# Rows of 132 columns for two pictures in device memory and for the strip tiles

## The chip, the cores and the metric

One core of one Trainium2 chip runs the whole program. The metric is the device time of one execution in microseconds, the median of several runs.

## The reference, cut to what matters

Two layers on four pictures of 96 channels and 128 x 128 points. The first layer is a window attention beside a depthwise 3 x 3 convolution, mixed by a gate and projected; the second is a depthwise convolution with four taps whose filter is computed from the picture's mean.

```python
x = layernorm2d(x0, ln_w, ln_b)
qk, vs = conv1x1(x, qk_w, qk_b), conv1x1(x, vs_w, vs_b)
local = depthwise3x3(vs, depth_w) + depth_b
v1, v2 = vs[:, :48], vs[:, 48:]
q, k, v1 = roll(q, -4, -4), roll(k, -4, -4), roll(v1, -4, -4)
y = roll(attention in 8 x 8 windows, 4 heads of 12 channels, +4, +4)
y = concatenate([y, v2])
s = (y + local).mean(axis=(2, 3))
ca = sigmoid(fu2(leaky_relu(fu1(s), 0.2)))
y = conv1x1(y * ca + local * (1 - ca), proj_w, proj_b) + x0
out = depthwise, 4 taps of a masked 3 x 3, filter from mean(y)
```

## The kernel before, in words

The pictures are worked through in strips of 8 rows, 16 strips to a picture and 64 in all (`NS`, `B`). A strip holds 16 windows of 8 x 8 points. The rows of the attention's strips lie 4 rows lower than those of the output's strips, because of the roll.

There are two stages, and they run interleaved. The attention stage takes strip t: it loads x, normalises it into `xn`, makes values, keys and queries, the scores, the softmax and the attention's output, and stores two pictures in device memory: `v_img` (the value picture, 96 channels, with a zero row above and below) and `y_img` (the attention's output, 48 channels). The output stage runs 17 strips later (`LAG`): it loads strip u = t - 17 of both pictures into `vin` (10 rows with a zero column at either side), `ycat` and `x0`, adds the nine taps and the projection up in PSUM, and applies the second layer to the strip `zs`. The gate and the filter of a picture need sums over the whole picture, so at the end of each picture two strips carry extra steps (the strips with `gate` and `gated`), a chain of small products and sums that goes back and forth between VectorE and TensorE.

So the program has three kinds of strips. The first 16 run the attention alone (the functions `alone`). Then 48 strips run both stages (`strip`). The last 17 strips run the output stage alone (`last` on VectorE).

There is no scheduler: on each engine the order of the work is written out by hand, as one list of calls per strip, and semaphores with counted values do the rest. The orders that matter here:

- ScalarE (ACT), `strip` at L827: the two exponentials `exps(t, 0)`, the two copies `vs_out` of the values with their bias, `y_out(t - 1)`, `exps(t, 1)`, the two `keys`, `rsqrt`, the two `queries`, then `tap0`, `sum_x`, `first`, `values`.
- TensorE (PE), `strip` at L624: `x_transposed`, `scores_transposed(k, 0)`, `vs_of`, `y_transposed(t - 1)`, `scores_transposed(k, 1)`, `keys_queries`, `values(t, k, 0)`, `rstd_rows`, then a wait for the keys and the queries (L651, L652), `scores(1 - k, 0)` (L493), `project`, `scores(1 - k, 1)`, `values(t, k, 1)`, `project`, `v_transposed`, `project_mixed`.
- VectorE (DVE), `strip` at L1175: `finish`, statistics, five tap sums `mix`, `divide`, `normalise`, `maxima`, taps of the second layer `l1`.
- GpSimd (POOL), `to_image` at L410: eight small copies that turn the values from window order into rows (`vrow`), and one for the edge columns.
- SyncE (SP) issues all the DMAs.

The names that the change touches: `load_x` (L265) loads x rolled by four columns, so that each half strip takes two DMAs, one of 124 columns and one of 4. `windows` (L463) reads windows out of `xn`. `yq` holds the attention's output in window order with 2 x 48 channels for two groups of windows; `y_transposed` (L513) transposes it to 96 partitions, group 0 on partitions 0 to 47 and group 1 on 48 to 95; `y_out` (L757) copies that to `ybuf` with two instructions, one for each `wi`, each with a sum for the picture's mean into `ystat`; `store_y` (L282) writes `ybuf` to `y_img` with four DMAs in runs of 32 columns. `load_strip` (L292) reads `y_img` back with two DMAs, rolled by four columns. `mean_y` (L1051) sums `ystat`, and the product with `fold` (L667, issued by L574) adds the two groups of partitions. Two things on PE wait for `y_out`: `values(t, k, 0)` through `y1_done` (L525), and nothing else; but `exps(t, 1)` and all that follows it on ACT stand behind `y_out` in ACT's list.

Of the kernel before, what the change touches and what calls it, by code (L numbers as in the profile page):

```python
# [31 lines left out]
SH = WS // 2  # L32
# [12 lines left out]
VW = HD + 1  # L45

# [32 lines left out]
def program(nc, x, out, w):  # L79
    ctx = ExitStack()  # L80
    with ctx:
# [40 lines left out]
        xn = sb("xn", [C, WS, W])  # L122
# [7 lines left out]
        idle = sb("idle", [C, 1])  # L130
        rec = sb("rec", [128, 2, 16])
        yq = sb("yq", [128, 4, 2, A])
        vrow = sb("vrow", [C, 2, WS, W])
        ybuf = sb("ybuf", [C, 2, WS, 2, 4 * WS])

        vstat = sb("vstat", [C, 2 * (B * NS + 2)])
        ystat = sb("ystat", [C, 2 * B * NS])
# [14 lines left out]
        vin = sb("vin", [C, 2, WS + 2, W + 2])  # L152
        ycat = sb("ycat", [C, 2, WS, W])
        x0 = sb("x0", [C, 2, WS, W])
        mb = sb("mixed", [C, 2, WS, W])
# [3 lines left out]
        v_img = nc.dram_tensor("v_img", (B + 1, C, H + 2, W), F32, kind="Internal").ap()  # L159
        y_img = nc.dram_tensor("y_img", (B, A, H, W), F32, kind="Internal").ap()  # L160
# [34 lines left out]
        xn_done = sem("xn_done")  # L195
        xsum_done = sem("xsum_done")
# [36 lines left out]
        N_MID, MID_STEPS, MID_PE = 28 + len(PE_TAPS), 6, 7  # L233
# [21 lines left out]
        def _(sp):  # L255
# [26 lines left out]
            def store_y(s, par):  # L282
                b, i = image_of(s)
                at = [held(rows_of(i, c)) for c in range(2)]
                sp.wait_ge(y1_done, 2 * (s + 1))
                for c in range(2):
                    rows = y_img[b, :, bass.ds(at[c], 4), :].rearrange("c r (w g x) -> c r w g x", w=2, g=2)
                    for g in range(2):
                        sp.dma_start(rows[:, :, :, g, :],
                                     ybuf[g * A:(g + 1) * A, par, 4 * c:4 * c + 4, :, :]).then_inc(y_stored[par], 16)  # L290

            def load_strip(u, par, prev, gate):  # L292

                b, j = image_of(u)
                before, top, below = held(u - 1), held(j * WS), held(j * WS + 1)
                if prev:
                    sp.wait_ge(z_done, before)
                sp.dma_start(vin[:, par, :, 1:1 + W], v_img[b, :, bass.ds(top, WS + 2), :]).then_inc(vin_loaded[par], 16)
                sp.dma_start(ycat[A:C, par, :, :], v_img[b, A:C, bass.ds(below, WS), :]).then_inc(ycat_loaded[par], 16)
                rows = y_img[b, :, bass.ds(top, WS), :]  # L300
                if gate is not None:
                    sp.wait_ge(y_stored[1], FREE + 64 * (NS // 2) * (gate + 1))
                sp.dma_start(ycat[0:A, par, :, SH:W], rows[:, :, 0:W - SH]).then_inc(ycat_loaded[par], 16)
                sp.dma_start(ycat[0:A, par, :, 0:SH], rows[:, :, W - SH:W]).then_inc(ycat_loaded[par], 16)
# [16 lines left out]
            for b in range(B):  # L321
                for row in (0, H + 1):
                    sp.dma_start(v_img[b, :, row, :], zs[:, 0, 0:W]).then_inc(rim_stored, 16)
# [8 lines left out]
            def strip(h, k, attend=True, y=True, ahead=False, prev=False, older=False, gate=None):  # L332
# [4 lines left out]
                if gate is not None:  # L337
                    sp.wait_ge(y_stored[0], FREE + 64 * (NS // 2) * (gate + 1))
                    sp.wait_ge(v_stored[0], 32 * ((gate + 1) * (NS // 2) + 1))
                    sp.wait_ge(v_stored[1], 32 * (gate + 1) * (NS // 2))  # L340
                    for at, row in ((0, H), (1, 1)):
                        sp.dma_start(erow[:, at, :], v_img[gate, :, row, :]).then_inc(erow_loaded, 16)
# [50 lines left out]
        def _(pool):  # L393
            for at, value in ((0, LN_EPS), (1, BN_EPS)):
                nc.gpsimd.memset(eps[:, at:at + 1], value).then_inc(eps_set, 1)
            for t in (w_qk[:], place[:], vd[:], edge[:], idle[:], zs[:], q_scale[:],
                      vin[:, 0, :, 0], vin[:, 0, :, W + 1], vin[:, 1, :, 0], vin[:, 1, :, W + 1]):
# [12 lines left out]
            def to_image(s, par, free):  # L410
# [5 lines left out]
                for c in range(2):  # L416
# [5 lines left out]
                    put(rows[:, :, SH:SH + W // 2], of[:, 0])  # L422
# [889 lines left out]
```

## Time and profile before, and how to read it

| | us |
|---|---|
| median of 3 runs | 1599.65 (1597.12 to 1601.26) |
| the profiled execution, its own time | 1606.61 |
| span of the profiled execution | 1604.8 |
| busy in it: PE, DVE, ACT, POOL | 1524.8, 1335.9, 791.9, 222.7 |
| mean granted clock of TensorE, share of the full 2.4 GHz | 0.977 |

The profile shows one execution. Busy times are sums over the span; the kernel's stages have different limits, so a share is only of use for a stage. A row of the timeline gives the start in us from the span's beginning, the time it covers, the engine, the line, the operation with its output and inputs, and how many instructions are merged (x4); in brackets stands the idle time of the engine before it and what ended that. SPq is SyncE's queue, its rows are the issues of DMAs. PEld is the load of weights into TensorE. ACTIVATION_READ_ACCUMULATOR is the second half of an ACT instruction that also sums.

### The profile page before, as it was taken

The page shows a single profiled execution, that of the slowest core. Times are in us where ns is not written, and L with a number is a line of the kernel's source. Part 1 is how long each engine was busy: PE and PEld are TensorE (multiplying, and loading weights), DVE is VectorE, ACT ScalarE, POOL GpSimd, SP SyncE. Part 2 cuts the span into 40 slices and gives each one's busy share as a digit, 9 for nine tenths or more (in the row PEclk, how much of TensorE's full clock was granted, in tenths as well). Part 3 has the DMA queues.
Part 4 walks back from the last instruction along what each step waited for, and adds up shares of the span by engine and source line. Part 5 has one row for each costly group of instructions (what it writes and reads, how often), then busy time and mean ns, then how long its engine had stood idle before and what let it go on. Part 6 is the DMA issues. An engine that isn't in the chain of part 4 may idle for free.

```text
span 1604.8 us, 34488 instructions
## 1 busy us (share of the span) xinstructions
PE 1524.8 (95%) x10619; PEld 932.8 (58%) x10619; DVE 1335.9 (83%) x2450; ACT 791.9 (49%) x1819; POOL 222.7 (14%) x675
## 2 busy tenths in 40 slices
PE   5999999899999999999999999989999999969997
PEld 3676767666656666556656665556566665523332
DVE  3565656559999999889999999889999999889998
ACT  2555555435555555536555556545555565512221
POOL 1111111101111111201111111111111111100000
PEclk9999999869999999989999999999999999989999
DMA  2232222426655665455566655664566555657874
GB/s 57 52 71 56 68 59 65 85 58 125 132 112 108 124 128 126 110 98 118 115 115 130 123 117 110 121 121 92 118 133 123 112 111 121 134 104 157 161 161 109
DMA packets 360943, 174.15 MB, mean 109 GB/s; under 512 B 267760, under 2 KB 333064, under 8 KB 360904
## 3 DMA queue, kind: packets, MB, share of 16 engines
q1 hardware_dynamic: 360904, 173.69, 52.6%
q8 instruction: 17, 0.28, 0.1%
q14 instruction: 22, 0.18, 0.0%
HBM read 108.85 MB, written 63.70 MB: 108 GB/s over the span
## 4 chain that ended last, share of the span: by engine, by line
PE 85%; DVE 8%; issue 3%; ACT 1%; DMA 1%; SPq 0%; DVEq 0%; ACTq 0%
PE banks_g L586 14%; PE banks_s L497 8%; PE banks_g L472 8%; PE banks_t L533 7%; PE banks_a L533 7%; PE banks_g L480 6%; PE banks_g L593 6%; PE banks_t L505 6%; PE banks_g L588 6%; PE banks_t L459 4%; PE banks_t L586 3%; PE banks_a L447 2%; PE banks_a L486 2%; DVE zs L1143 2%; PE banks_a L517 2%
## 5 line engine op out<-in xcount | busy, mean ns | idle before, releaser
L1120 DVE SCALAR_TENSOR_TENSOR mixed<-vin,c_pack,mixed 96x1024 f32<-96x1024 f32 x352 | 453.8, 1289 | 6.4
L586 PE MATMUL banks_g<-vin,proj_t 96*96 96x512 f32 x512 | 250.1, 616 | 3.6 <-DVE st L1094 3.6
L1131 DVE SCALAR_TENSOR_TENSOR oo<-zs,l_w,oo 96x1024 f32<-96x1024 f32 x192 | 245.5, 1279 | 8.9 <-ACT oo L805 3.3
L755 ACT ACTIVATE vd<-banks_a 64x192 f32<-64x192 f32 x260 | 86.9, 334 | 307.3 <-PE banks_a L486 302.4
L922 DVE TENSOR_REDUCE mx<-banks_s 128x8 f32<-128x512 f32 x260 | 167.1, 684 | 39.7 <-PE banks_s L497 36.3
L769 ACT ACTIVATE pt<-banks_t 128x512 f32<-128x512 f32 x256 | 138.6, 593 | 97.4 <-PE banks_t L505 97.4
L420 POOL COPY vrow<-vw 96x16 f32<-96x16 f32 (+2 forms) x520 | 177.3, 390 | 0.0
L415 POOL TENSOR_TENSOR idle<-idle 96x1 f32<-96x1 f32 x65 | 13.4, 207 | 1163.1 <-ACT vw L746 1163.1
L497 PEld LDWEIGHTS banks_s<-km,qd 64*128 64x128 f32 x2080 | 132.6, 195 | 56.1 <-DVE mx L922 38.3
L497 PE MATMUL banks_s<-km,qd 64*128 64x128 f32 x2080 | 157.8, 293 | 4.8 <-DVE mx L922 3.3
L795 ACT ACTIVATE mixed<-vin,c_pack 96x1024 f32<-96x1024 f32 x64 | 73.5, 1149 | 166.8 <-DMA vin<-v_img 166.8
L505 PE MATMUL banks_t<-qd,km 64*128 64x128 f32 x2048 | 152.2, 289 | 1.4 <-DMA qd<-nmx 1.4
L893 DVE BATCH_NORM_STATS2 bn<-banks_a 128x6 f32<-128x96 f32 x528 | 98.7, 247 | 58.0 <-PE banks_a L447 56.2
L533 PEld LDWEIGHTS banks_a<-vd,pt 128*128 128x128 f32 x1024 | 120.8, 194 | 41.1 <-issue 41.1
L472 PE MATMUL banks_g<-xn,c_pack 96*96 96x512 f32 x260 | 133.5, 638 | 9.2 <-DVE zs L1143 8.3
L505 PEld LDWEIGHTS banks_t<-qd,km 64*128 64x128 f32 x2048 | 127.4, 191 | 19.1 <-issue 8.7
L805 ACT ACTIVATE oo<-zs,c_pack,l_w 96x1024 f32<-96x1024 f32 x64 | 79.1, 1235 | 118.9 <-DVE zs L1143 118.9
L586 PEld LDWEIGHTS banks_g<-vin,proj_t 96*96 96x96 f32 x512 | 78.8, 167 | 98.3 <-issue 89.5
L533 PE MATMUL banks_t<-vd,pt 128*128 128x52 f32 x1024 | 128.9, 280 | 0.0
L480 PE MATMUL banks_g<-xn,w_qk 96*32 96x512 f32 x1040 | 128.6, 613 | 0.0
L533 PE MATMUL banks_a<-vd,pt 128*128 128x52 f32 x1024 | 127.3, 278 | 0.0
L533 PEld LDWEIGHTS banks_t<-vd,pt 128*128 128x128 f32 x1024 | 120.7, 194 | 7.9 <-issue 0.2
(134 smaller groups left out, 1909.7 us busy)
## 6 DMA issues: line engine op xcount, KB each, us to landing
vin<-v_img SPq DMA_DIRECT2D x64, 480.0 KB, 5.7
v_img<-vrow SPq DMA_DIRECT2D x130, 192.0 KB, 2.2
xc<-in_x SPq DMA_DIRECT2D x134, 186.0 KB, 5.6
x<-in_x SPq DMA_DIRECT2D x64, 384.0 KB, 7.0
out<-oo SPq DMA_DIRECT2D x64, 384.0 KB, 3.0
y_img<-ybuf SPq DMA_DIRECT2D x256, 48.0 KB, 1.7
ycat<-v_img SPq DMA_DIRECT2D x64, 192.0 KB, 5.4
ycat<-y_img SPq DMA_DIRECT2D x64, 186.0 KB, 5.5
```

The lines of the kernel that those rows point to most:

```text
L420: nc.gpsimd.tensor_copy(dst.rearrange("c r (p x) -> c p r x", x=min(WS, src.shape[-1])), src).then_inc(vrow_done, 1)
L472: mm(banks_g[:C, w, :], wvs[:], windows(w), start=True, stop=True).then_inc(vs_done, 1)
L480: last = mm(banks_g[q0:q0 + 32, at, :], w_qk[:, kind, t, :], windows(w), start=True, stop=True, tile_position=(0, q0))
L497: last = mm(banks_s[:, t, e * 128:(e + 1) * 128], operand(qd, t, k, p), operand(km, t, k, p), start=True, stop=True, tile_position=(64 * t ...
L505: last = mm(banks_t[:, n, e * 128:(e + 1) * 128], operand(km, n, k, p), operand(qd, n, k, p), start=True, stop=True, tile_position=(64 * n ...
L533: last = mm(bank[:, at:at + 52], pt[:, 2 * half + n, e * 128:(e + 1) * 128], vd[:, k, 4 * half + e, n, :, :, :].rearrange("k w h d -> k (w ...
L586: mm(z, proj_t[:, n, :], vin[:, par, at:at + 4, 1 + dw:1 + dw + W], start=n == 0, stop=False)
L769: fn(pt[:, 2 * r + n, :], banks_t[:, n, :], ACT.Exp).then_inc(pt_done, 1)
L893: last = v.bn_stats(bn6[:, c, j, :], ps_ln[:, j * C:(j + 1) * C])
L922: v.tensor_reduce(mx[:, n, :, 4 * r:4 * r + 4].rearrange("q h e -> q e h"), banks_s[:, n, :].rearrange("q (e h k) -> q e h k", h=2, k=K), ...
L1120: v.scalar_tensor_tensor(out=mb[:, par, :, :], in0=vin[:, par, 1 + dh:1 + dh + WS, 1 + dw:1 + dw + W], scalar=depth_w[:, DVE_TAPS[m]:DVE_T ...
L1131: v.scalar_tensor_tensor(out=oo[:, par, :, :], in0=zs[:, at:at + WS, 1 + dw:1 + dw + W], scalar=l1_w[:, n:n + 1], in1=oo[:, par, :, :], op ...
```

## The change

Rows get a pitch of 132 columns (`PITCH = W + SH`) in `xn`, `vrow`, `ybuf`, `vin`, `ycat`, `mixed` and in the two pictures in device memory, so that a strip tile and the rows that are stored and loaded have the same layout, and one channel of a DMA is one contiguous run.

- x is loaded as it lies, with one DMA for each half strip. GpSimd copies the first four columns of `xn` behind the last (`wrap`, new), and `windows` reads from column 4 on. `vs_of` waits for that copy.
- The value picture's row has a zero column ahead and three behind; `vin` is loaded with one DMA of whole rows, and its columns are no longer set to zero by themselves. `vrow`, `yq`, `ystat` and a new tile `nil` are set to zero at the start.
- `yq` gets 64 columns for each group, so that the transposed output has group 0 on partitions 0 to 47 and group 1 on 64 to 111. `y_out` copies it with four instructions, two for each group, all to partitions 0 to 47 of `ybuf`, in turned columns, and a fifth for four columns that wrap round.
- `store_y` takes two DMAs in place of four, the load of `y_img` one in place of two.
- `ystat` has four sums for each strip on 48 partitions, and the product with `fold` goes; `mean_y`, `squeeze_in` and `leaky` count one step less to PE.

The core of the diff:

```diff
+PITCH = W + SH
+YO = 5
             def load_x(b, i, c):
-                rows, strip = x[b, :, bass.ds(rows_of(i, c), 4), :], chunk(xc[:, c, :])
-                sp.dma_start(strip[:, :, 0:W - SH], rows[:, :, SH:W]).then_inc(x_loaded[c], 16)
-                sp.dma_start(strip[:, :, W - SH:W], rows[:, :, 0:SH]).then_inc(x_loaded[c], 16)
+                sp.dma_start(chunk(xc[:, c, :]), x[b, :, bass.ds(rows_of(i, c), 4), :]).then_inc(x_loaded[c], 16)
...
                 for c in range(2):
-                    rows = y_img[b, :, bass.ds(at[c], 4), :].rearrange("c r (w g x) -> c r w g x", w=2, g=2)
-                    for g in range(2):
-                        sp.dma_start(rows[:, :, :, g, :],
-                                     ybuf[g * A:(g + 1) * A, par, 4 * c:4 * c + 4, :, :]).then_inc(y_stored[par], 16)
+                    sp.dma_start(y_img[b, :, bass.ds(at[c], 4), :],
+                                 ybuf[:, par, 4 * c:4 * c + 4, :]).then_inc(y_stored[par], 16)
...
-                sp.dma_start(ycat[0:A, par, :, SH:W], rows[:, :, 0:W - SH]).then_inc(ycat_loaded[par], 16)
-                sp.dma_start(ycat[0:A, par, :, 0:SH], rows[:, :, W - SH:W]).then_inc(ycat_loaded[par], 16)
+                sp.dma_start(ycat[0:A, par, :, :], y_img[b, :, bass.ds(top, WS), :]).then_inc(ycat_loaded[par], 16)
...
-                      vin[:, 0, :, 0], vin[:, 0, :, W + 1], vin[:, 1, :, 0], vin[:, 1, :, W + 1]):
+                      vrow[:], yq[:], ystat[:], nil[:]):
...
+            def wrap(s):
+                pool.wait_ge(xn_done, 2 * (s + 1))
+                nc.gpsimd.tensor_tensor(xn[:, :, W:PITCH], xn[:, :, 0:SH], nil[:], ALU.add).then_inc(xw_done, 1)
...
             def vs_of(s):
-                pe.wait_ge(xn_done, 2 * (s + 1))
+                pe.wait_ge(xw_done, s + 1)
...
-                    last = nc.tensor.transpose(ps_o[:C, e * 128:(e + 1) * 128],
+                    last = nc.tensor.transpose(ps_o[:, e * 128:(e + 1) * 128],
...
             def y_out(t, par, before):
                 act.wait_ge(yt_done, t + 1)
-                src = ps_o[:C, :].rearrange("c (e w r x) -> c e w r x", e=4, w=2, x=WS)
-                for wi in range(2):
-                    dst = ybuf[:, par, :, wi, :].rearrange("c r (e x) -> c e r x", x=WS)
-                    fn(dst, src[:, :, wi, :, :], ACT.Copy,
-                       accum_out=ystat[:, bass.ds(2 * t + wi, 1)]).then_inc(y1_done, 1)
+                for g in range(2):
+                    src = ps_o[64 * g:64 * g + A, :].rearrange("c (e w r x) -> c e w r x", e=4, w=2, x=WS)
+                    for wi in range(2):
+                        at = SH + wi * W // 2 + g * W // 4
+                        dst = ybuf[:, par, :, at:at + W // 4].rearrange("c r (e x) -> c e r x", x=WS)
+                        fn(dst, src[:, :, wi, :, :], ACT.Copy,
+                           accum_out=ystat[0:A, bass.ds(4 * t + 2 * g + wi, 1)]).then_inc(y1_done, 1)
+                fn(ybuf[:, par, :, 0:SH], src[:, 3, 1, :, SH:WS], ACT.Copy).then_inc(y1_done, 1)
...
-                if gate is not None:
-                    one_column(gate, fold[:], st[:, 0:1], 0, C, 1)
```

## Rows read from the trace of the kernel before

**Rows 1.** The page, part 4: the chain that ended last, by engine

```profile
PE 85%; DVE 8%; issue 3%; ACT 1%; DMA 1%; SPq 0%; DVEq 0%; ACTq 0%
```

**Rows 2.** Busy time by stage: stretch, length, each engine, PE's clock, DMA share, GB/s

```profile
40.00:296.00 256.00, 238.31 (x2308) 180.13 (x2306) 151.24 (x428) 137.59 (x376) 35.30 (x160) 1.00 0.27 62
296.00:350.00 54.00, 49.98 (x307) 34.86 (x306) 28.27 (x90) 22.91 (x55) 5.43 (x20) 0.65 0.43 87
350.00:660.00 310.00, 307.87 (x2249) 188.86 (x2250) 284.08 (x491) 174.51 (x399) 52.97 (x140) 1.00 0.57 117
...
1435.00:1605.00 170.00, 159.80 (x379) 60.68 (x377) 156.74 (x128) 37.37 (x37) 0.00 (x0) 0.98 0.70 145
```

**Rows 3.** Timeline of ACT in one strip with both stages

```profile
883.40 0.37 ACT L763 ACTIVATE ybuf<-banks_a 96x256 f32<-96x256 f32 x1
883.66 0.19 ACT L763 ACTIVATION_READ_ACCUMULATOR ybuf<-banks_a  x1
883.75 0.37 ACT L763 ACTIVATE ybuf<-banks_a 96x256 f32<-96x256 f32 x1
...
884.18 1.08 ACT L769 ACTIVATE pt<-banks_t 128x512 f32<-128x512 f32 x2
885.68 1.45 ACT L733 ACTIVATE km<-banks_g,k_bias,k_scale 128x512 f32<-128x512 f32 x2 [0.41 <-PE banks_g L480]
...
887.54 1.43 ACT L739 ACTIVATE qd<-banks_g,q_bias,q_scale 128x512 f32<-128x512 f32 x2
```

**Rows 4.** Timeline of PE in the same strip, before and after ACT's queries

```profile
886.40 1.99 PE L533 MATMUL banks_a<-vd,pt 128*128 128x52 f32 x16
...
889.19 1.16 PE L497 MATMUL banks_s<-km,qd 64*128 64x128 f32 x16
```

**Rows 5.** The page, part 2: DMA packets of the whole span

```profile
DMA packets 360943, 174.15 MB, mean 109 GB/s; under 512 B 267760, under 2 KB 333064, under 8 KB 360904
```

**Rows 6.** Timeline of SP's queue at the start

```profile
1.48 0.42 SPq L267 DMA_DIRECT2D xc<-in_x  x1
...
2.98 0.48 SPq L268 DMA_DIRECT2D xc<-in_x  x1
```

**Rows 7.** The chain of waits at the start: start, length, what

```profile
3.50 2.52 DMA ln_pack<-in_ln_pack
...
10.26 0.15 DVE place L963
```

**Rows 8.** Timeline of POOL at the start

```profile
2.73 1.94 POOL L398 MEMSET zs<- 96x2210 f32 x1
...
5.46 0.53 POOL L407 MEMSET q_scale<- 32x1 f32 x4
```

**Rows 9.** Timeline of all engines: from the normalised strip to its first reader

```profile
864.64 1.26 POOL L426 COPY ecol<-vw 96x16 f32 x1
...
868.12 1.28 DVE L914 TENSOR_TENSOR xn<-banks_t,xc 96x512 f32<-96x512 f32 x2
...
880.65 1.96 PE L472 MATMUL banks_g<-xn,c_pack 96*96 96x512 f32 x4
```

**Rows 10.** Groups of instructions by line and shape: count, busy us, mean ns

```profile
L769 ACT ACTIVATE pt<-banks_t 128x512 f32<-128x512 f32 x256 | 138.6, 593 | 97.4 <-PE banks_t L505 97.4
...
L755 ACT ACTIVATE vd<-banks_a 64x192 f32<-64x192 f32 x260 | 86.9, 334 | 307.3 <-PE banks_a L486 302.4
```

**Rows 11.** Timeline of ACT in a strip of the attention alone, and four copies merged

```profile
201.21 1.41 ACT L755 ACTIVATE vd<-banks_a 64x192 f32<-64x192 f32 x4 [5.48 <-PE banks_a L486]
...
204.97 1.08 ACT L769 ACTIVATE pt<-banks_t 128x512 f32<-128x512 f32 x2 [0.16 <-PE banks_t L505]
206.85 1.45 ACT L739 ACTIVATE qd<-banks_g,q_bias,q_scale 128x512 f32<-128x512 f32 x2 [0.79 <-PE banks_g L480]
...
209.36 1.06 ACT L769 ACTIVATE pt<-banks_t 128x512 f32<-128x512 f32 x2
```

**Rows 12.** Timeline of PE: the end of an attention strip, and the last picture's gate

```profile
210.57 1.04 PE L459 MATMUL banks_t<-ident,rstd 128*96 128x128 f32 x8 [1.01 <-ACT pt L769]
...
1412.62 0.48 PE L574 MATMUL banks_s<-st,c_pack 96*96 96x1 f32 x2 [6.83 <-DVE st L1053]
```

More of the change, by code:

```diff
@@ L284, in store_y, with strip_of @@
                 at = [held(rows_of(i, c)) for c in range(2)]
[L285 removed]
+                sp.wait_ge(y1_done, YO * (s + 1))
                 for c in range(2):
[L287 to L290 removed]
+                    sp.dma_start(y_img[b, :, bass.ds(at[c], 4), :],
+                                 ybuf[:, par, 4 * c:4 * c + 4, :]).then_inc(y_stored[par], 16)
             def load_strip(u, par, prev, gate):
                 b, j = image_of(u)
[L295 removed]
+                before, top = held(u - 1), held(j * WS)
+                first, below = held(j * WS * PITCH + 1), held(j * WS * PITCH + PITCH + 1)
+                def strip_of(c0, c1, at):
+                    flat = v_img[b, c0:c1, :, :].rearrange("c r x -> c (r x)")
+                    return flat[:, bass.ds(at, WS * PITCH)].rearrange("c (r x) -> c r x", x=PITCH)
                 if prev:
                     sp.wait_ge(z_done, before)
[L298 to L300 removed]
+                sp.dma_start(vin[:C, par, :, :], v_img[b, :, bass.ds(top, WS + 2), :]).then_inc(vin_loaded[par], 16)
+                sp.dma_start(ycat[A:C, par, :, :], strip_of(A, C, below)).then_inc(ycat_loaded[par], 16)
                 if gate is not None:
[L302 to L304 removed]
+                    sp.wait_ge(y_stored[1], FREE + 32 * (NS // 2) * (gate + 1))
+                sp.dma_start(ycat[0:A, par, :, :], y_img[b, :, bass.ds(top, WS), :]).then_inc(ycat_loaded[par], 16)
                 if prev:
@@ L337, in strip @@
                 if gate is not None:
-                    sp.wait_ge(y_stored[0], FREE + 64 * (NS // 2) * (gate + 1))
+                    sp.wait_ge(y_stored[0], FREE + 32 * (NS // 2) * (gate + 1))
                     sp.wait_ge(v_stored[0], 32 * ((gate + 1) * (NS // 2) + 1))
@@ L341, in strip @@
                     for at, row in ((0, H), (1, 1)):
-                        sp.dma_start(erow[:, at, :], v_img[gate, :, row, :]).then_inc(erow_loaded, 16)
+                        sp.dma_start(erow[:, at, :], v_img[gate, :, row, 1:1 + W]).then_inc(erow_loaded, 16)
                 if y:
@@ L524, in values @@
                     if not first:
-                        pe.wait_ge(y1_done, 2 * t)
+                        pe.wait_ge(y1_done, YO * t)
                 else:
@@ L587, in project @@
                        start=n == 0, stop=False)
-                mm(z, proj_c[:], ycat[:, par, 4 * c:4 * c + 4, :], start=False, stop=False)
+                mm(z, proj_c[:], ycat[:, par, 4 * c:4 * c + 4, 0:W], start=False, stop=False)
             def project_mixed(u, par, last):
@@ L592, in project_mixed @@
                 for c in range(2):
-                    done = mm(z_bank(par, last)[:C, c, :], proj_m[:], mb[:, par, 4 * c:4 * c + 4, :], start=False, stop=True)
+                    done = mm(z_bank(par, last)[:C, c, :], proj_m[:], mb[:, par, 4 * c:4 * c + 4, 0:W], start=False, stop=True)
                 done.then_inc(z_done, 1)
@@ L672, in strip @@
                 if gate is not None:
-                    one_column(gate, fu1T[:], st[:, 5:6], 1, R, 2)
+                    one_column(gate, fu1T[:], st[:, 5:6], 1, R, 1)
                 if gated is not None:
@@ L683, in strip @@
                 if gate is not None:
-                    one_column(gate, fu2T[:], tr[:, 1:2], 2, C, 3)
+                    one_column(gate, fu2T[:], tr[:, 1:2], 2, C, 2)
             alone(0, 0, y=False)
@@ L1051, in mean_y @@
             def mean_y(b):
-                dve.wait_ge(y1_done, 2 * NS * (b + 1))
-                to_pe(b, v.tensor_reduce(s(0), ystat[:, bass.ds(2 * NS * b, 2 * NS)], AX.X, ALU.add))
+                dve.wait_ge(y1_done, YO * NS * (b + 1))
+                step(v.tensor_reduce(s(0), ystat[:, bass.ds(4 * NS * b, 4 * NS)], AX.X, ALU.add))
             def squeeze_in(b):
                 settle(b)
-                dve.wait_ge(mid_pe, MID_PE * b + 1)
-                step(v.tensor_scalar(s(4), one[:C, 0:1], s(8), 1.0 / PX, ALU.add, ALU.mult))
+                step(v.tensor_scalar(s(4), s(0), s(8), 1.0 / PX, ALU.add, ALU.mult))
                 settle(b)
```

76 lines of the change are left out of this document (42 added, 34 removed).

## The prediction

> **What bounds the kernel now.** I read the chain of waits first, summed by engine: TensorE (PE) carries 85% of it, DMA 1%, ScalarE (ACT) 1% [rows 1]. Then busy time by stage [rows 2], because a share of the span mixes stages. From 40 to 296 us attention runs alone, PE is busy for 238 of 256 us, and the chain leaves it in each strip for a detour over VectorE (DVE) and ACT. From 350 to 660 us both stages run: PE is busy for 307.87 of 310 us, DVE for 284. Fourteen strips fit there, and two more stretches of fourteen look the same, so 42 strips have PE full. In the tail from 1435 us DVE is busy for 157 of 170 us: its eight passes over a strip set the pace. DMA engines are busy for a quarter to 0.7 of each stage, and nowhere the limit.
>
> Third, the timeline of one of those 42 strips, to see what PE barely gets in time. ACT has a share of only 56% there, yet works in a fixed order. In it `y_out` ends, `exps(t, 1)` follows at once, then the keys start after 0.41 us of idle time, then the queries end at 887.54 + 1.43 = 888.97 [rows 3]. PE's scores, which read them, start at 889.19 [rows 4], 0.22 us later, with PE's preceding work just done. So ACT's list has some slack ahead of the keys and next to none behind them.
>
> **The change part by part.**
>
> *DMA.* 267,760 of 360,943 packets are under 512 bytes [rows 5]; x's pieces, `ybuf`'s runs of 128 bytes and the rolled load of `y_img` make up most of these, and they become runs of about 2 to 5 KB. DMA time will fall a good deal. Worth: 0 in the steady stages, because no strip waits there for a landing on its chain (DMA 1%, [rows 1]); the cover is PE's and DVE's own work. SP issues five DMAs fewer in a strip; nothing that SP issues is late.
>
> *The start.* SP issues four loads of x, then the pack on which the chain stands at 3.50 us [rows 6, 7]. Two loads fewer at (2.98 - 1.48) / 3 = 0.50 us each: -1.0 us. POOL's new zeros are 2112 + 512 + 256 + 32 elements a partition; by the 2210 elements in 1.94 us that is some 2.5 us, so POOL's set-up ends at 5.99 + 2.5 = 8.5 us [rows 8]. DVE first asks for it at 10.26 - 1.0 = 9.3 us [rows 7]: covered by 0.8 us. In the first strip `wrap` stands openly between normalise and `vs_of`: 0.2 us for a small POOL instruction and one more semaphore, estimate +0.3. Sum: -0.7 us.
>
> *`wrap` in the other strips.* `xn` is ready at 868.12 + 1.28 = 869.40 and read at 880.65 [rows 9]: 11.2 us for one small copy behind `to_image`. Even the slowest small POOL copy, 1.26 us beside DVE's passes [rows 9], fits nine times. Cost 0.
>
> *PE.* Four transposes load 128 columns where they loaded 96. Bounds: nothing, because each streams 128 columns as before and the load runs beside it, up to a few hundredths each. I take 0. Reading windows from column 4 of a 132 pitch: the taps already read shifted rows of 130 at the normal pace; 0.
>
> *`y_out` on ACT.* Here the cost lies. Today two copies, each with a read of its sum, take 883.75 - 883.40 = 0.35 us a pair [rows 3], although the two parts last 0.37 and 0.19: each instruction starts about 0.1 us before the one ahead has ended. After: four pairs and a copy of 32 elements. I take a pair on 48 partitions to cost what one on 96 does, since a copy of 64 x 192 lasts 0.334 [rows 10], near the 0.37 less 64 elements: 2 x 0.355 = 0.71 more. The small copy: two exponentials of 512 elements last 1.08 together [rows 3] and one 0.593 [rows 10], so a step of 0.49; the 256 of `ybuf` step 0.26; that is 0.9 ns an element, and 0.07 for 32 elements. Sum with full overlap 0.78 us.
>
> Does the overlap hold? The only ACT instructions here that change their partitions from one to the next are the four of L755, from and to halves of 64: each lasts 0.334, four take 1.41 [rows 10, 11], so a step of 0.36. The overlap of 0.1 is gone and 0.025 of gap is added: 0.12 each. In the new `y_out` the source moves from partition 0 to 64 between the groups and back before `exps`; the target stays. L755 changes its target each time, so it doesn't say which of the two counts. Ends: 0.78 us (only targets count), and, with no overlap anywhere, 4 x (0.37 + 0.20 + 0.05) + 0.2 - 0.71 = 1.98. I take two drains, 0.78 + 0.24 = 1.02, as L755 is the nearest row.
>
> Slack ahead of the keys: 0.41 idle, 0.1 for the overlap that a chained instruction has, and 0.07 that `exps` waits today: 0.58. So keys and queries come 1.02 - 0.58 = 0.44 us later. Of the 0.22 us between the queries' end and PE's start, 0.15 is the step from ACT's end to PE in the nearest row (209.36 + 1.06 to 210.57, [rows 11, 12]); slack 0.07 to 0.22, I take 0.12. PE is late by 0.44 - 0.12 = 0.32 us in each strip. Nothing gives it back: DVE's `finish`, and with it the next strip, starts from PE's last product. 42 x 0.32 = +13.4 us. `y1_done` costs nothing: y ends at about 884.1 + 1.0, its reader starts at 886.40 [rows 4].
>
> *The same in attention alone.* There `exps(t, 0)` waits 0.16 and the queries 0.79 us [rows 11], with 0.1 of overlap about the 1.02; PE idles 1.01 later in the strip anyway [rows 12]. Cost 0.
>
> *`fold`.* At the last gate PE waits 6.83 us for `mean_y` before `fold` [rows 12], and `project` stands behind it. Afterwards `project` runs in that gap, but DVE still carries the chain, and PE idles longer ahead of its next product. Between -2 and +2; I take 0.
>
> Sum: -0.7 + 13.4 = +12.7 us, on the profiled execution 1606.61 + 12.7 = 1619.3. That execution is 7.0 us above the median of the runs, 1599.65; the forecast for the median is **1612 us**.
>
> **The rivals.**
>
> *Full overlap, no difference.* Only targets count, ACT's block grows by 0.78, the queries come 0.20 later, PE 0.08: 42 x 0.08 - 0.7 = +2.7, **1602 us**. For it: target and source both move in L755's middle step, and its step is no longer than the other two. Against it: both move in none of the rows without the target. The Trainium skill, "ScalarE: Activation LUTs", section "What ACT_TABLE_LOAD costs", states that back-to-back ACTIVATEs overlap by about 93 ns, with no exception for partitions; by that rule this rival holds. The pair in rows 3 agrees with it, the four copies in rows 11 don't.
>
> *More drains.* The read of a sum may have partitions of its own, so that each step from group 1's source to its sum drains. Six drains: 0.78 + 0.72 - 0.58 - 0.12 = 0.80 a strip, +33 us, **1632**; no overlap at all: 1.98 - 0.70 = 1.28, +53, **1653**. Against the latter: 96 and 128 partitions alternate now without a drain.
>
> *Faster, through the clock.* Around the first gate, 296 to 350 us, PE's granted clock averages 0.65 [rows 2], so part of that stretch runs at 1.2 GHz, after waits of PE in the gate's chain. At the full clock it would take up to 0.35 x 54 = 19 us less. One step less in the chain could keep the clock up; it decides if the granted clock there rises above 0.9. With the full-overlap cost: 1602 - 19 = **1583**. Against it: `fold` isn't what PE waits for there, and the wait ahead of the drop is DVE's maxima. In the attention stage an idle 1 us in each strip leaves the clock at 1.00.
>
> *It doesn't do what it says*: if the packets stayed small, time would be as forecast, as DMA isn't in the sum.
>
> **How the numbers follow.** A measurement of this kernel can tell 0.3%, 4.8 us, from no change. Two drains (about +12.7) 0.44; full overlap 0.34, nearly all within 0.3%; more drains 0.14; faster through clock or gates 0.07, the small rest spread. So faster 0.08, same 0.34, slower 0.58. The range reaches from the full-overlap case with all its slack, 1599 - 1 = 1598, to six drains, 1633; left out are the clock case and no overlap at all. The forecast's own range, by the slack's ends (0.07 to 0.22), is 1608 to 1615.
>
> **What would show it.** In a steady strip: five y copies in about 1.7 us; no idle time ahead of the keys (0.41 before); scores starting 0.15 to 0.2 after the queries' end with an idle PE ahead of them; the strip longer by 0.3 us; PE's share from 350 to 660 us below 99%. Packets under 512 bytes fall to under a tenth. `wrap` done ten us ahead of its reader. Wrong I am if the keys still wait for PE, if steady strips keep their length, or if the difference lies at the gates.

## The result, and the profile after

The kernel after takes 1612.76 us (median of 7 runs, 1608.79 to 1620.32), the kernel before beside it 1603.62 us: ratio 1.0063, 95% interval 1.0035 to 1.0091. A second comparison, told below, gave 1615.26 against 1599.90 us: 1.0091, interval 1.0066 to 1.0116. So the change costs 9 to 15 us, more than the 0.3% that can be told from no change.

The page of the kernel after: the DMA packets and the chain that ended last.

```profile
DMA packets 72143, 177.10 MB, mean 109 GB/s; under 512 B 12176, under 2 KB 16040, under 8 KB 72104
...
PE 85%; DVE 9%; issue 4%; ACT 1%; DMA 1%; SPq 0%; DVEq 0%; ACTq 0%; POOL 0%; POOLq 0%
```

The change does what it says: four fifths fewer packets, and those under 512 bytes fall from 267,760 to 12,176 [rows 5]. DMA's share of the chain stayed at 1% [rows 1].

Busy time by stage of the kernel after (columns as in rows 2):

```profile
40.00:296.00 256.00, 238.11 (x2319) 180.10 (x2317) 152.32 (x432) 151.84 (x453) 40.19 (x176) 1.00 0.22 63
...
350.00:660.00 310.00, 303.73 (x2222) 187.28 (x2221) 278.57 (x481) 185.82 (x467) 64.74 (x154) 1.00 0.46 117
```

In the attention alone ACT has 14 us more work and PE's figure is as in [rows 2]. In the stretch with both stages ACT has 11 us more, the DMA share fell from 0.57 to 0.46, and PE lost 4 of its 308 busy us. What PE waits for there is one view further, the sum of its waits by what ended them (total us, times, longest). First the kernel before, then the kernel after, 350 to 660 us:

```profile
PE banks_g L472 <- DVE zs L1143: 2.1, 7, 0.3
```

```profile
PE banks_s L511 <- issue: 4.1, 14, 0.3
PE banks_g L486 <- DVE zs L1157: 2.1, 7, 0.3
```

Fourteen new waits of 0.29 us, one in each strip, ahead of the scores; the old one, for `zs` in every second strip, is unchanged. "Issue" names no releaser; the timeline does. It shows ACT of the kernel after in one such strip, with the lines of PE and POOL that are used here and below:

```profile
887.85 0.36 ACT L777 ACTIVATE ybuf<-banks_a 48x256 f32<-48x256 f32 x1
...
888.21 0.37 ACT L777 ACTIVATE ybuf<-banks_a 48x256 f32<-48x256 f32 x1
888.47 0.20 ACT L777 ACTIVATION_READ_ACCUMULATOR ybuf<-banks_a  x1
888.69 0.38 ACT L777 ACTIVATE ybuf<-banks_a 48x256 f32<-48x256 f32 x1
...
889.07 0.37 ACT L777 ACTIVATE ybuf<-banks_a 48x256 f32<-48x256 f32 x1
...
889.43 0.18 ACT L779 ACTIVATE ybuf<-banks_a 48x32 f32<-48x32 f32 x1
889.64 1.08 ACT L784 ACTIVATE pt<-banks_t 128x512 f32<-128x512 f32 x2
890.61 1.45 ACT L745 ACTIVATE km<-banks_g,k_bias,k_scale 128x512 f32<-128x512 f32 x2
...
892.47 1.43 ACT L751 ACTIVATE qd<-banks_g,q_bias,q_scale 128x512 f32<-128x512 f32 x2
...
894.00 1.16 PE L511 MATMUL banks_s<-km,qd 64*128 64x128 f32 x16 [0.29 <-issue]
...
896.04 0.25 POOL L436 TENSOR_TENSOR xn<-xn,nil 96x32 f32<-96x32 f32 x1 [3.58 <-DVE xn L929]
...
907.86 1.93 PE L486 MATMUL banks_g<-xn,c_pack 96*96 96x512 f32 x4 [0.31 <-DVE zs L1157]
```

Read it beside [rows 3, 4]. The copies follow each other by 0.36 us while they read the same group of partitions; from the second to the third, where the source moves from partition 0 to 64, the step is 0.48, and the third begins after the read ahead of it has ended (888.47 + 0.20 = 888.67). The same between the small copy (889.43 + 0.18 = 889.61) and the exponentials at 889.64. The keys no longer wait for PE: the 0.41 us ahead of them are gone. The queries end at 893.90, and PE's scores start 0.10 us later after an idle 0.29. (The last line is a product that waits for `zs` by 0.31, the old wait.)

### The profile page after: what moved, and what is told of

Read it like the earlier page. It is cut to its first block, busy times and chain, and to the rows that moved or that the text cites. A ratio compares the mean times of both kernels' runs of the same rounds, so it can differ in the third digit from the quotient of the medians.

```text
span 1618.5 us, 34138 instructions
## 1 busy us (share of the span) xinstructions
PE 1526.5 (94%) x10611; PEld 933.6 (58%) x10611; DVE 1332.2 (82%) x2450; ACT 847.7 (52%) x2139; POOL 269.4 (17%) x741
## 2 busy tenths in 40 slices
DMA packets 72143, 177.10 MB, mean 109 GB/s; under 512 B 12176, under 2 KB 16040, under 8 KB 72104
## 4 chain that ended last, share of the span: by engine, by line
PE 85%; DVE 9%; issue 4%; ACT 1%; DMA 1%; SPq 0%; DVEq 0%; ACTq 0%; POOL 0%; POOLq 0%
PE banks_g L600 14%; PE banks_s L511 8%; PE banks_g L486 8%; PE banks_t L547 7%; PE banks_a L547 7%; PE banks_g L494 6%; PE banks_g L607 6%; PE banks_t L519 6%; PE banks_g L602 6%; PE banks_t L473 4%; PE banks_t L600 3%; PE banks_a L461 2%; PE banks_a L500 2%; DVE zs L1157 2%; PE banks_a L531 2%
## 5 line engine op out<-in xcount | busy, mean ns | idle before, releaser
L424 POOL COPY vrow<-vw 96x16 f32<-96x16 f32 (+2 forms) x520 | 182.5, 405 | 0.0
```

Of the source, the lines that this page charges most:

```text
L424: nc.gpsimd.tensor_copy(dst.rearrange("c r (p x) -> c p r x", x=min(WS, src.shape[-1])), src).then_inc(vrow_done, 1)
```

## Where the time came from

A strip is measured here from the start of its first scores to the same two strips on, since strips alternate. Kernel before: 889.19 [rows 4] and, two strips on, 933.60; kernel after: 894.00 and 939.15.

```profile
933.60 1.16 PE L497 MATMUL banks_s<-km,qd 64*128 64x128 f32 x16
```

```profile
939.15 1.16 PE L511 MATMUL banks_s<-km,qd 64*128 64x128 f32 x16 [0.29 <-issue]
```

So 44.41 us for a pair before and 45.15 after: +0.37 a strip (22.04 and 22.37 became 22.40 and 22.74). The same starts, taken over the whole span, split the difference. Two pairs of profiled executions are shown, the first from the comparison above, the second from both kernels profiled again (runs `e8_before_again` and `e9_after_again` below):

| stretch | before | after | diff. | before again | after again | diff. |
|---|---|---|---|---|---|---|
| start to first strip's scores | 32.06 | 31.67 | -0.39 | 31.87 | 31.54 | -0.33 |
| from there to second strip's scores | 16.69 | 15.53 | -1.16 | 15.59 | 16.83 | +1.24 |
| attention alone, 15 strips | 239.35 | 239.34 | 0.0 | 239.45 | 239.37 | -0.1 |
| first gate, 3 strips | 78.74 | 77.90 | -0.8 | 68.47 | 68.30 | -0.2 |
| steady, 39 strips | 865.37 | 879.96 | **+14.6** | 865.46 | 880.00 | **+14.5** |
| other gates, 6 strips | 156.86 | 158.08 | +1.2 | 156.78 | 157.78 | +1.0 |
| rest | 215.72 | 216.02 | +0.3 | 215.68 | 216.57 | +0.9 |
| span | 1604.8 | 1618.5 | +13.7 | 1593.3 | 1610.4 | +17.1 |

What stands out in both pairs is the steady strips: 39 by 0.374 us. The second row differs by 1.1 to 1.3 us between two executions of the same kernel, so it says nothing of the change; in that strip PE's products still come down to the shorter time of later strips (16 of L497 take 2.08 us in the first strip's scores, 1.16 in the second's).

## The experiments

The theory (A): `y_out` on ACT is the whole cost; its steps lose their overlap where the source's partitions change (a drain, as the prediction calls it), and what of the longer block doesn't fit into ACT's slack of 0.7 us is paid in each strip. Rivals: rows, loads and packets matter; any longer block is paid in full; the wait lies elsewhere.

**One part alone.** `e1_y_only`: of the change, the attention's output alone (y's tiles and picture, `y_out`, `fold` no longer applied).

```diff
-                src = ps_o[:C, :].rearrange("c (e w r x) -> c e w r x", e=4, w=2, x=WS)
-                for wi in range(2):
...
+                for g in range(2):
+                    src = ps_o[64 * g:64 * g + A, :].rearrange("c (e w r x) -> c e w r x", e=4, w=2, x=WS)
+                    for wi in range(2):
...
+                fn(ybuf[:, par, :, 0:SH], src[:, 3, 1, :, SH:WS], ACT.Copy).then_inc(y1_done, 1)
```

> The kernel before with the change's part for y alone (y_out, yq, ybuf, y_img, ycat, no fold); x is loaded rolled and v_img and vin keep their old rows. Theory A (ACT's longer y block, two drains in it, makes keys and queries late, and PE waits for the queries): a pair of strips with both stages takes 45.1 us as after the change, not 44.4; keys start without idle time ahead of them; 13 to 16 us above before (ratio about 1.009). Theory B (the cost comes from GpSimd's new copy ahead of vs_of, or from reading and writing rows of 132): 44.4 us for a pair, ratio 1.000.

Measured: 1610.93 against 1601.09 us, ratio 1.0073 (1.0045 to 1.0101). Scores two strips apart in it:

```profile
884.90 1.16 PE L499 MATMUL banks_s<-km,qd 64*128 64x128 f32 x16 [0.29 <-issue]
...
930.05 1.16 PE L499 MATMUL banks_s<-km,qd 64*128 64x128 f32 x16 [0.29 <-issue]
```

45.15 us, the pace of the whole change. `e2_x_and_v`: the rest of the change without y.

```diff
-YO = 5
+YO = 2
...
-                                 ybuf[:, par, 4 * c:4 * c + 4, :]).then_inc(y_stored[par], 16)
+                                     ybuf[g * A:(g + 1) * A, par, 4 * c:4 * c + 4, :, :]).then_inc(y_stored[par], 16)
```

> The change without its part for y: x loaded as it lies with GpSimd's copy, v_img, vin, vrow and mixed with rows of 132, y as before. Theory A: 44.4 us for a pair of strips with both stages, as before; 1 to 3 us below before from the start (two loads of x fewer ahead of the first product), ratio 0.998 to 1.000. Theory B: 45.1 us for a pair, ratio about 1.008.

Measured: 1604.66 us, ratio 1.0025 (0.9997 to 1.0053).

```profile
876.32 1.16 PE L515 MATMUL banks_s<-km,qd 64*128 64x128 f32 x16
...
920.74 1.16 PE L515 MATMUL banks_s<-km,qd 64*128 64x128 f32 x16
```

44.42 us, the pace of before. The y part is the whole loss. The gain of 1 to 3 us that A expected of the rest isn't seen in the median; its execution ended 3.75 us later than the one before (219.47 us after the last strip's scores). That was asked of x alone, below.

**The drains alone.** `e3_same_half` is the kernel after with both groups read from partitions 0 to 47; it leaves out half of the attention's output. All counts, sizes and targets stay.

```diff
-                    src = ps_o[64 * g:64 * g + A, :].rearrange("c (e w r x) -> c e w r x", e=4, w=2, x=WS)
+                    src = ps_o[0:A, :].rearrange("c (e w r x) -> c e w r x", e=4, w=2, x=WS)
```

> The changed kernel, but y_out reads both groups from partitions 0 to 47 (the second group's columns are then a copy of the first's, so that half of the attention's output is left out). The same five instructions, no change of partitions between them. Theory A: the two gaps of 24 ns and the lost overlap go, the y block takes 0.24 us less, PE waits 0.24 us less in a strip: a pair takes 44.7 us, the time lies 9 to 10 us below the changed kernel (ratio to before 1.000 to 1.003). If only the number of instructions counts: 45.1 us for a pair, ratio to before 1.006.

Measured: 1597.79 us, ratio 0.9985 (0.9958 to 1.0013). ACT's timeline and PE's scores in it:

```profile
895.00 0.37 ACT L777 ACTIVATE ybuf<-banks_a 48x256 f32<-48x256 f32 x1
...
895.36 0.37 ACT L777 ACTIVATE ybuf<-banks_a 48x256 f32<-48x256 f32 x1
...
896.07 0.19 ACT L779 ACTIVATE ybuf<-banks_a 48x32 f32<-48x32 f32 x1
896.14 1.07 ACT L784 ACTIVATE pt<-banks_t 128x512 f32<-128x512 f32 x2
```

```profile
878.06 1.16 PE L511 MATMUL banks_s<-km,qd 64*128 64x128 f32 x16
...
922.61 1.16 PE L511 MATMUL banks_s<-km,qd 64*128 64x128 f32 x16
```

The second group now follows the first by 0.36, the exponentials follow the small copy by 0.07, and the pair of strips takes 44.55 us: 0.07 a strip over before, where the full-overlap rival had 0.08. So five narrow copies cost nearly nothing in the strip; the other 0.30 is the two changes of partition. The 3 us that 0.07 makes over the 39 strips don't show in the median, which lies 3 us below that of the kernel before (the interval ends at 1.0013, where 1.0019 was due).

`e4_turns` takes the groups in turn, so that the source moves four times instead of twice.

```diff
-                for g in range(2):
-                    src = ps_o[64 * g:64 * g + A, :].rearrange("c (e w r x) -> c e w r x", e=4, w=2, x=WS)
-                    for wi in range(2):
+                for wi in range(2):
+                    for g in range(2):
+                        src = ps_o[64 * g:64 * g + A, :].rearrange("c (e w r x) -> c e w r x", e=4, w=2, x=WS)
```

> The changed kernel with the four copies of y_out in another order: group 0, group 1, group 0, group 1. The same instructions and the same result, but the source changes its partitions four times in place of two. Theory A: 0.24 us more in the y block, a pair of strips takes 45.6 us, 10 us above the changed kernel (ratio to before about 1.012). If only the number of instructions counts: 45.1 us for a pair and 1.006.

Measured: 1627.97 us, ratio 1.0156 (1.0100 to 1.0212). ACT's timeline and PE's scores:

```profile
886.20 0.36 ACT L777 ACTIVATE ybuf<-banks_a 48x256 f32<-48x256 f32 x1
...
886.68 0.38 ACT L777 ACTIVATE ybuf<-banks_a 48x256 f32<-48x256 f32 x1
...
887.18 0.38 ACT L777 ACTIVATE ybuf<-banks_a 48x256 f32<-48x256 f32 x1
...
887.68 0.38 ACT L777 ACTIVATE ybuf<-banks_a 48x256 f32<-48x256 f32 x1
```

```profile
892.63 1.16 PE L511 MATMUL banks_s<-km,qd 64*128 64x128 f32 x16 [0.31 <-issue]
...
938.34 1.16 PE L511 MATMUL banks_s<-km,qd 64*128 64x128 f32 x16 [0.31 <-issue]
```

Steps of 0.48 to 0.50 at each move, and 45.71 us for the pair: two more drains cost 0.28 a strip over the kernel after, 0.14 each.

**The slack.** `e5_twice` is the kernel before with its two copies done twice, the second time into a spare tile: a longer block without a change of partitions.

```diff
+                for wi in range(2):
+                    fn(again[:, wi, :].rearrange("c (e r x) -> c e r x", e=4, x=WS), src[:, :, wi, :, :], ACT.Copy,
+                       accum_out=spare[:, bass.ds(2 * t + wi, 1)]).then_inc(y1_done, 1)
```

> The kernel before, with the two copies of y_out done a second time into a spare tile: four pairs on 96 partitions and no change of the source's partitions. It leaves nothing of the computation out. Theory A (only the lost overlap at a change of the source's partitions makes the strip longer; four pairs alone fit into ACT's slack): the block grows by 2 x 0.355 = 0.71 us, 0.58 + 0.12 of it lie in the slack, so a strip grows by 0.01 us, 22.05 and 22.38 us, the idle time ahead of the keys is 0, and the whole gains or loses under 1 us. Theory B (any longer block of ACT is paid in full): +0.71 x 42 = +30 us. Theory C (the slack ahead of the keys is the 0.41 us alone that the trace shows, and the 0.12 behind them): 0.71 - 0.53 = 0.18 in a strip, +7.6 us.

Measured: 1601.22 against 1604.75 us, ratio 0.9985 (0.9954 to 1.0015).

```profile
899.08 0.37 ACT L765 ACTIVATE ybuf<-banks_a 96x256 f32<-96x256 f32 x1
...
900.51 1.09 ACT L774 ACTIVATE pt<-banks_t 128x512 f32<-128x512 f32 x2
```

```profile
882.50 1.16 PE L499 MATMUL banks_s<-km,qd 64*128 64x128 f32 x16
...
926.91 1.16 PE L499 MATMUL banks_s<-km,qd 64*128 64x128 f32 x16
```

44.41 us, as before, though `y_out` lasts 0.72 us more (899.08 to 900.51, 1.43, against the 0.71 of two pairs) and no idle time is left ahead of the keys. Theory B's +30 us and C's +7.6 are out. The slack is about 0.71 us.

**The rest.** `e6_x_only`: the kernel before with x loaded in whole rows and turned by GpSimd.

```diff
-                sp.dma_start(strip[:, :, 0:W - SH], rows[:, :, SH:W]).then_inc(x_loaded[c], 16)
-                sp.dma_start(strip[:, :, W - SH:W], rows[:, :, 0:SH]).then_inc(x_loaded[c], 16)
+                sp.dma_start(chunk(xc[:, c, :]), x[b, :, bass.ds(rows_of(i, c), 4), :]).then_inc(x_loaded[c], 16)
```

> The kernel before with x's part of the change alone (x loaded in whole rows, turned by GpSimd in its normalised tile). Theory A: steady strips as before, 22.04 and 22.37 us, three stretches of 13 strips at 288.4 to 288.6 us; the first strip's scores earlier by 1.5 to 1.9 us as in the change and in the run without y's part; the end 215.7 and gates 78.2 to 78.7 as before. Sum -1 to -2 us. Rival: x's whole rows load the tail, and the end is 219 us as in the run without y's part (219.47): then the sum is +2 us.

Measured: 1600.29 us, ratio 0.9976 (0.9952 to 1.0000), strips of 22.04 and 22.37, end 218.1 us. The 46.84, 48.75 and 47.46 us that the next expectation calls the first strip's scores are the second strip's; the first strip's start at 31.28 us here. It was timed again:

> The kernel before with x's part of the change alone, timed in more rounds, to see whether it beats both kernels. By the traces its steady strips are those of before and its first strip's scores come 0.6 to 1.9 us earlier (46.84 us against 48.75 and 47.46 in two looks at before): a ratio of 0.9988 to 0.9996, which is within 0.3% and not told from no change. A ratio whose interval lies wholly below 0.998 would say that something else is gained.

Measured: 1599.81 us, ratio 1.0000 (0.9983 to 1.0017), first strip's scores at 31.31, second strip's at 48.03, end 215.67. So the same kernel's first scores come at the same time to 0.03 us, while the second strip's move by 1.2 us and its end by 2.4 from one execution to another. The late end of `e2_x_and_v` needs no effect of the edit (`e5_twice`, with x loaded as before, ended 219.36 us after the last scores), and the 0.24% of `e6_x_only` didn't come again. What x's part does give is 0.6 to 0.8 us at the first scores (31.28 and 31.31 against 32.06 and 31.87), too little for a median to show; of that the whole change has 0.33 to 0.39 (table above), and what takes the rest isn't located.

`e7_wrap_by_pool`: the kernel after with the small fifth copy done by GpSimd.

```diff
-                fn(ybuf[:, par, :, 0:SH], src[:, 3, 1, :, SH:WS], ACT.Copy).then_inc(y1_done, 1)
...
+                nc.gpsimd.tensor_tensor(ybuf[:, par, :, 0:SH], ybuf[:, par, :, W:PITCH], nil[:A], ALU.add).then_inc(yw_done, 1)
```

> The kernel after, with the fifth copy of y_out (the wrap columns) taken from ACT and done by GpSimd in ybuf; the two changes of the source's partitions stay. Theory A (the small copy costs its step under overlap, 0.07 us, and the two drains stay): strips of 22.33 and 22.67 us, against 22.40 and 22.74; 42 x 0.07 = 3 us less than the kernel after. Rival (the second drain belongs to the small copy, whose step to the exponentials is 0.21 us in the trace): strips of 22.20 and 22.54, 8 us less. GpSimd's later end of y (some 2.5 us) is waited for by nobody in a steady strip.

Measured: 1611.45 us, ratio 1.0058 (1.0027 to 1.0089).

```profile
885.07 1.16 PE L520 MATMUL banks_s<-km,qd 64*128 64x128 f32 x16 [0.21 <-issue]
...
930.07 1.16 PE L520 MATMUL banks_s<-km,qd 64*128 64x128 f32 x16 [0.21 <-issue]
```

45.00 us a pair, 0.08 a strip less than the kernel after, as A had it: the small copy is worth its step of 0.07, and the drain behind it stays, whichever copy stands there.

**The kernels once more.** Both unchanged, to see what belongs to the execution.

> The kernel before, profiled once more. Open is whether the time around the first gate belongs to the kernel or to the execution: the strip there took 30.63 us with a granted clock of 0.50 from 320 to 340 us in the profile before, 20.5 to 21.4 us with a clock of 0.73 to 1.00 in the four experiments so far. If to the execution, this look may show either, and a look at 21 us settles it; the steady strips are 22.04 and 22.37 us in any case. If to the kernel, it is 30 to 31 us again.

Measured: 1595.11 us in one run.

> The kernel after, profiled and timed once more. The three stretches of 13 steady strips grow by 4.8 to 5.0 us each in the profile (14.6 in all) and the start gives 1.6 back: a ratio of about 1 + 13 / 1602 = 1.008; the medians so far say 1.0063 with an interval from 1.0035 to 1.0091. The strip at the first gate took 29.04 us in the profile after; if its clock belongs to the execution, this look may show 20 to 26, as the kernel before did when it was profiled again (30.63, then 20.55). Steady strips of 22.40 and 22.74 us in any case.

Measured: 1615.26 against 1599.90 us, ratio 1.0091 (1.0066 to 1.0116). The 1.6 us at the start didn't come again: the first strip's scores were 0.33 us earlier, the second strip's 0.91 later. The clock at the first gate, 330 to 340 us, from busy time by stage: before, before again, after, after again.

```profile
330.00:340.00 10.00, 10.00 (x54) 6.57 (x54) 5.54 (x14) 5.94 (x16) 2.91 (x9) 0.50 0.77 162
```

```profile
330.00:340.00 10.00, 10.00 (x78) 7.03 (x78) 8.50 (x16) 3.95 (x9) 0.00 (x0) 1.00 0.99 203
```

```profile
330.00:340.00 10.00, 10.00 (x50) 6.40 (x50) 6.11 (x15) 6.12 (x13) 0.38 (x4) 0.50 0.72 184
```

```profile
330.00:340.00 10.00, 10.00 (x80) 7.29 (x80) 7.97 (x14) 4.41 (x10) 0.92 (x2) 1.00 0.83 208
```

Both kernels show both levels there, 1.2 and 2.4 GHz, and the strip at the gate goes with it: 30.63 and 20.55 us before, 29.04 and 21.36 after. So up to 10 us there belong to the execution. Spans of two single executions can't be compared to better than that. The attention alone and the 39 steady strips can: they repeated to 0.1 us in both kernels (in `e7_wrap_by_pool` one of the three steady stretches ran 1.2 us longer than the other two).

**A repair.** If only the place of the block costs time, it should be free where ACT stands idle. `e11_y_first` is the kernel after with the last strip's y moved ahead, on PE and on ACT.

```diff
                 if attend:
+                    if y:
+                        y_transposed(t - 1)
                     x_transposed(t + 2, 0)
...
+                if y:
+                    y_out(t - 1, 1 - k, h - 1 + k)
                 if attend:
                     exps(t, 0)
                     vs_out(t + 1, 0)
                     vs_out(t + 1, 1)
-                if y:
-                    y_out(t - 1, 1 - k, h - 1 + k)
-                if attend:
                     exps(t, 1)
```

> The kernel after with the last strip's y moved forward in the strips that run both stages: on PE its four transposes stand ahead of the first x_transposed, on ACT y_out stands ahead of exps(t, 0), where ACT sat idle for 1.91 us. All five copies and both changes of the source's partitions stay. Theory A (the drains cost time only because the block stood between the values and the exponentials, with 0.71 us of slack): the block still lasts 1.7 to 1.8 us, but it fills ACT's idle time; keys wait for PE again by about 0.4 us, strips are 22.04 to 22.15 and 22.37 to 22.5, the three stretches of 13 take 288.4 to 290 us each, and the ratio is 0.998 to 1.002. Rival (the exponentials that follow y_out come later by more than PE's slack behind them, 0.4 us, or PE's shifted transposes wait for the values' copies): strips keep 22.4 and 22.74 or more, and the ratio stays at 1.006 to 1.009.

Measured: 1591.75 against 1604.88 us, ratio 0.9919 (0.9892 to 0.9945): faster than both kernels. ACT's timeline, PE's scores and busy time by stage:

```profile
896.41 0.38 ACT L779 ACTIVATE ybuf<-banks_a 48x256 f32<-48x256 f32 x1 [1.10 <-PE banks_a L531]
...
898.22 1.08 ACT L786 ACTIVATE pt<-banks_t 128x512 f32<-128x512 f32 x2
...
902.13 1.45 ACT L747 ACTIVATE km<-banks_g,k_bias,k_scale 128x512 f32<-128x512 f32 x2 [0.41 <-PE banks_g L494]
```

```profile
883.62 1.16 PE L511 MATMUL banks_s<-km,qd 64*128 64x128 f32 x16
...
927.67 1.16 PE L511 MATMUL banks_s<-km,qd 64*128 64x128 f32 x16
```

```profile
350.00:660.00 310.00, 310.00 (x2271) 190.62 (x2271) 285.27 (x494) 187.31 (x469) 59.89 (x154) 1.00 0.47 120
```

The block is as long as in the kernel after, 1.81 us (896.41 to 898.22), the keys wait for PE by 0.41 again, and the drains cost nothing. The pair takes 44.05 us, 0.36 less than before: A had expected no more than before's pace, and 0.998 for the ratio at best. The list of PE's waits is empty in this stretch. The 0.3 us for `zs` in every second strip is gone too, since the y transposes (0.6 us, which don't need `zs`) now stand ahead of the product that does. Of the 13 us between the medians 6.5 lie in the 39 steady strips (858.9 against 865.4 us) and 2.5 in the six strips of the later gates (154.3 against 156.9); the rest isn't located, and the kernel before's own median went from 1599.90 to 1604.88 us between the comparisons here. The gain isn't the change's doing as far as this goes, so the same move was put into the kernel before.

> The kernel before with the same move of the last strip's y (transposes first on PE, y_out first on ACT), none of the change. In the run before this one the move took away two waits of PE: the 0.29 us in every strip that the change had added, and the 0.3 us for zs in every second strip, which the kernel before has too. Theory A (the two waits are independent; with both gone PE is the bound and the change itself is worth only its start): strips of 22.02 us throughout, stretches of 13 strips at 286.3 us, 39 x (22.205 - 22.02) = 7 us less than before, a ratio of 0.992 to 0.996, not more than 2 us above the run before this one. Rival (the larger gain, a ratio of 0.992 where 7 us of steady strips give 0.9955, belongs to the change's wider rows once ACT is out of the way): the ratio here is 0.995 to 0.998 and its interval lies above 0.992.

Measured: 1595.18 against 1600.61 us, ratio 0.9958 (0.9939 to 0.9977).

```profile
881.69 1.16 PE L497 MATMUL banks_s<-km,qd 64*128 64x128 f32 x16
...
925.76 1.16 PE L497 MATMUL banks_s<-km,qd 64*128 64x128 f32 x16
```

44.07 us a pair: the faster pace is the move's. Over 39 strips the two moved kernels differ by 0.6 us (859.5 against 858.9). The medians differ by 3.4 us, more than A's 2, and the ratio lies in the ranges of both theories, so whether the wider rows are worth something once ACT is out of the way stays open.

## Why the prediction was right

*What bounds the kernel*: right for the steady strips, and with one omission. PE's 307.87 of 310 us [rows 2] were read as full. The missing 2.13 us are the seven waits for `zs`, and they could be had: 6 us over the 39 steady strips, as the last two runs show.

*`y_out` on ACT*: the mechanism as forecast, two drains. Five copies with full overlap were put at +0.78 us and measured 0.79 (894.64 to 896.14 in `e3_same_half`, 1.50, against the 0.71 of two pairs). A drain was put at 0.12, from L755's steps; here it is 0.14 to 0.15. So the block grew by 1.08 instead of 1.02 (887.85 to 889.64, 1.79).

*The slack* was put at 0.58 + 0.12 = 0.70 and is 0.71: `e5_twice` adds 0.72 and loses under 0.01 a strip, `e3_same_half` adds 0.79 and loses 0.07, the kernel after adds 1.08 and loses 0.37. `e7_wrap_by_pool` adds 1.00 and loses 0.30, `e4_turns` adds 1.35 and loses 0.65. Five kernels, one number, 0.70 to 0.72. The 0.12 between the queries and PE is the 0.22 before less the 0.10 after; the prediction chose it between 0.07 and 0.22 with no row for it, so that it fits to 0.01 is partly luck, and its sign of 0.15 to 0.2 us at that place came out as 0.10.

*The strip*: +0.32 forecast, +0.37 measured; the 0.05 are the two drains' price, the term that was too small. It made 39 x 0.374 = 14.6 us, the forecast's 42 x 0.32 = 13.4. The six strips at the later gates gave 1.0 to 1.2.

*The start* was put at -0.7 and measured -0.39 and -0.33, by the first strip's scores in the two pairs of executions. Two loads fewer bring VectorE's first step on the pack 0.80 us earlier, where 1.0 was forecast (10.26 in [rows 7], 9.46 after); `wrap` takes 0.40 back, where 0.3 was forecast: PE waits 1.27 us for it, against 0.87 for the normalised strip before. First the kernel before, then the kernel after, its chain and its timeline:

```profile
18.16 3.70 PE L472 MATMUL banks_g<-xn,c_pack 96*96 96x512 f32 x4 [0.87 <-DVE xn L914]
...
32.06 2.08 PE L497 MATMUL banks_s<-km,qd 64*128 64x128 f32 x16
```

```profile
9.46 0.15 DVE place L978
```

```profile
17.76 3.70 PE L486 MATMUL banks_g<-xn,c_pack 96*96 96x512 f32 x4 [1.27 <-POOL xn L436]
...
31.67 2.08 PE L511 MATMUL banks_s<-km,qd 64*128 64x128 f32 x16
```

So the sign was right and the size half; it is 0.3 us of 1600.

*What was put at 0.* The attention alone: 239.34 against 239.35 us, although ACT does 14 us more. `wrap`: POOL ends one at 896.04 + 0.25 = 896.29 and PE reads it at 907.86, 11.6 us later. DMA: its share of the steady stretch fell by a fifth, from 0.57 to 0.46, and with x and v alone changed the pace stayed at 44.42 us a pair. PE's four transposes of the output take 0.60 us in both kernels. `fold`: PE waits 6.96 us at the last gate (at 1428.76 us), 6.83 before [rows 12], now for another sum, as forecast.

*The rivals.* Full overlap is what `e3_same_half` makes of the change, and its pace was the rival's; the change itself drains twice. The Trainium skill ("ScalarE: Activation LUTs", section "What ACT_TABLE_LOAD costs"), by whose overlap of about 93 ns this rival held, agrees with `e3_same_half` and `e5_twice`, where copies overlap by 0.09 to 0.10 us, and not with the steps at which the source moves: there a gap of 0.02 us stands in place of the overlap. The reads of the sums add no drains of their own: the second group's two copies follow each other by 0.38 us (888.69 and 889.07). (With no overlap at all the prediction's terms add up to 1.97, not 1.98 us; nothing hangs on it.) The clock at the first gate is at either level in both kernels, so no gain is the change's.

*The total*: 1612 was forecast for the median and 1612.76 measured, 1619.3 for a profiled execution and 1620.32 measured. Part of that nearness is luck. The kernel before took 1603.62 us beside it, not the 1599.65 that the forecast starts from, so the medians differ by 9.1 us where 12.7 were forecast (by 15.4 in the second comparison); and both profiled executions happened to have the low clock at the first gate. The better test is the 0.05 us in the strip.

## What to carry to other kernels

Here four fifths fewer packets gained nothing in the steady strips, because no transfer ended a wait of PE there. Ask first whether one does, which engine's list the rearrangement will lengthen instead, and how much slack that list has at that place. The idle time in the trace alone understates it, even on an engine that is busy for half its time: 0.41 us of idle time ahead of the keys, 0.10 for the overlap of a chained instruction, 0.07 that the exponentials waited and 0.12 of the gap to the reader made 0.70, and 0.70 to 0.72 were measured. When a block doesn't fit, look for an earlier place in the hand-written order with its inputs ready: here that made the cost in the strip vanish, and the same move covered an older wait of another engine.

## What the runs showed of the hardware

ACT's overlap between instructions is lost when the source alone moves from partition 0 to 64 or back, with the target staying: 0.14 us a change, shown by two, none and four changes in a strip. The four copies of L755 lose it too: two of their three steps move the target alone and one moves both, and each step is 0.35 to 0.36 us at 0.334 of duration [rows 10, 11], so a move of both costs no more than a move of the target. A copy of 48 partitions takes as long as one of 96: 0.36 to 0.38 us for 256 elements in both. Which clock PE is granted around the first gate differs between executions of one kernel, after waits of the same length (the kernel before waits there for VectorE's maxima, 1.90 us in the execution whose granted clock is 0.50 from 330 to 340 us, the level of 1.2 GHz, and 1.89 in the one where it is 1.00); what decides it is not shown here. Whether a smaller move of the source, within a half, loses the overlap too wasn't tried.
